# Graph attention on one core: softmax inside tiles of 128 edges, with 0/1 matrices that ScalarE forms, in place of scans that run over all edges

## What is computed

```
L0:  dinv = rsqrt(degree);  w = dinv[row] * dinv[col]
     h = x;  x_out = 0.1 x;  five times: h = segment_sum(h[col] * w, row);  x_out += 0.18 h
     x = layernorm(x + x_out @ W0.T + b0)
L1:  q = (x @ Wq)                                     # n x 8 heads x 8
     k = ((x[src] * (sh @ Wang_k.T)) @ Wlin_k) * (relu(ea @ W1k + b1k) @ W2k)     # e x 8 x 8
     v = ((x[src] * (sh @ Wang_v.T)) @ Wlin_v) * (relu(ea @ W1v + b1v) @ W2v)     # e x 8 x 16
     alpha = einsum('ehq,qk,ehk->eh', q[dst], Wdot, k)
     attn  = softmax of alpha over the edges of one dst, per head
     x = layernorm(x + segment_sum(attn * v, dst) @ Wout)
```

## Time and profile before

| | |
|---|---|
| median of 3 runs | 7642.49 us (7631.2 to 7643.73) |
| profiled execution, its span | 7626.3 us |
| instructions | 100,942 |
| PE busy | 5985.3 us (78%) |
| VectorE (DVE) busy | 4953.3 us (65%) |
| GpSimd (POOL) busy | 3561.9 us (47%) |
| ScalarE (ACT) busy | 2725.1 us (36%) |
| `edge_attention`, first transpose to the issue of the last store | 3311.0 to 7451.0 us |

### The profile page before, as it was taken

How to read it: one execution, slowest core, us unless ns; L and a number is a source line. 1 busy time by engine, 2 the same in 40 slices (tenths; PEclk the granted TensorE clock), 3 DMA queues, 4 the chain that set the end, 5 groups by cost and what they waited for, 6 DMA issues and landing times. The chain is left out here.

```text
span 7626.3 us, 100942 instructions
## 1 busy us (share of the span) xinstructions
PE 5985.3 (78%) x25186; PEld 2930.0 (38%) x25186; DVE 4953.3 (65%) x6867; ACT 2725.1 (36%) x5068; POOL 3561.9 (47%) x3216
## 2 busy tenths in 40 slices
PE   3444599999999998358888888888888888888883
PEld 3444444444444444323333333333333333333331
DVE  5555611111111112369999999999999999999994
ACT  3443411111111111234444444444444444444441
POOL 2222110000000000267777777777777777877773
PEclk7666799999999999578988888888898899998885
DMA  5666769687877867034444443444434444443441
GB/s 104 104 102 104 109 224 314 207 289 235 262 251 240 280 215 267 21 83 112 111 111 110 110 113 108 112 111 110 112 110 109 113 110 110 112 112 108 113 104 39
DMA packets 1158275, 1100.52 MB, mean 144 GB/s; under 512 B 569810, under 2 KB 997180, under 8 KB 1158092
## 3 DMA queue, kind: packets, MB, share of 16 engines
q1 hardware_dynamic: 753548, 752.46, 36.0%
q10 hardware_dynamic: 344208, 218.52, 8.9%
q0 software_dynamic: 60336, 127.10, 6.2%
HBM read 791.60 MB, written 305.95 MB: 144 GB/s over the span
## 5 line engine op out<-in xcount | busy, mean ns | idle before, releaser
L2025 POOL DMA_INDIRECT e_x_rows<-x_table,e_src_ix x1616 | 2007.2, 1242 | 525.8 <-issue 512.9
L1154 PE MATMUL acc<-t_ring,scaled 128*128 128x512 f16 (+1 forms) x9555 | 1966.5, 368 | 56.4 <-ACT scaled L1173 46.1
L1154 PEld LDWEIGHTS acc<-t_ring,scaled 128*128 128x128 bf16 x9555 | 907.4, 98 | 1100.9 <-issue 76.3
L2095 PE MATMUL e_b_gv<-e_prod,e_head_sum 64*128 64x512 f32 x808 | 524.4, 734 | 682.3 <-DVE e_x_gv L2206 679.2
L1250 POOL TENSOR_TENSOR less_two<-less_one,scaled 128x512 f32<-128x512 f32 (+1 forms) x65 | 71.9, 1106 | 1759.6 <-ACT scaled L1173 1759.6
L534 PE MATMUL lists_rows_ps<-lists_hot_lo,lists_hot_hi 128*128 128x196 fp8e4 x3200 | 436.9, 313 | 463.4 <-DVE lists_hot_hi L459 463.3
L2037 POOL TENSOR_TENSOR e_lift<-e_lift,e_top 128x512 f32<-128x512 f32 x404 | 577.1, 1429 | 31.7
L534 PEld LDWEIGHTS lists_rows_ps<-lists_hot_lo,lists_hot_hi 128*128 128x128 fp8e4 x3200 | 378.6, 122 | 517.9 <-DVE lists_hot_hi L459 482.4
L2053 PE MATMUL e_b_lk<-e_x_gk,e_wlin_k 128*64 128x512 f32 x808 | 576.8, 804 | 0.0
L2034 POOL TENSOR_TENSOR e_lift<-e_fresh,e_top 128x512 f32<-128x512 f32 x404 | 442.8, 1096 | 284.7 <-DVE e_top L2251 268.8
L2157 ACT COPY e_out_rows<-e_b_o 128x512 f32<-128x512 f32 x404 | 236.2, 585 | 871.9 <-PE e_b_gk L2105 871.9
(11 more groups left out here) (173 smaller groups left out, 8881.5 us busy)
## 6 DMA issues: line engine op xcount, KB each, us to landing
t_ring<-adjacency_half SPq DMA_DIRECT2D x245, 800.0 KB, 7.0
t_ring<-adjacency_half SPq DMA_DIRECT2D x245, 768.0 KB, 4.3
sums_table<-e_out_rows ACTq DMA_DIRECT2D x404, 272.0 KB
e_same_dst<-same_row SPq DMA_DIRECT2D x404, 256.0 KB, 3.7
adjacency_half<-lists_staged SPq DMA_DIRECT2D x196, 392.0 KB, 8.3
q_first<-hop_zeros_q ACTq DMA_DIRECT2D x101, 512.0 KB, 8.6
e_q_rows<-q_first SPq DMA_DIRECT2D x404, 128.0 KB
parts_sh<-e_part ACTq DMA_DIRECT2D x404, 64.0 KB, 4.4
```

The source lines that it names most:

```text
L1154: mm = nc.tensor.matmul(acc[c][:, 0:n], U[p][:, b, :], ring[m % RING][:, lo:lo + n], start=(b == 0 and p == 0), stop=(b == NB - 1 and p == 2),
L2025: nc.gpsimd.indirect_dma_start(x_rows[s][:, j, :], None, x1_table, bass.IndirectOffsetOnAxis(ap=src_ix[s][:, j:j + 1], axis=0)).then_inc(x ...
L2095: nc.tensor.matmul(b_gv[:], head_sum[:], prod[o][:], start=True, stop=True).then_inc(p_score, 1)
```

## The change

- Edges are taken in pairs of groups, group i of the first half of the edge list beside group i + 202 of the second half: 202 pairs (`N`), written out without a loop (`ITERATIONS`), the values running seven pairs behind (`LAG`). Work with 64 partitions is stacked, one group in the lower and one in the upper 64.
- Scores of four pairs (`BATCH`) are put on the 128 partitions (4 pairs x 4 tile positions x 8 heads) with two tiles of 128 edges along the free axis. Maximum and sum are found by scans inside one tile of 128 edges (`find_most` forward and backward, `add_weights` backward), 256 columns each per four pairs. The flags `neg` and `keep` come from two new tables in HBM.
- Values are formed with edges on partitions: `values` and `radial_values` are 8 matmuls of 128 columns each whose stationary operand is the edges' data, and VectorE multiplies straight from PSUM (`weigh`, `finish_values`).
- The sum over the edges of a segment inside a tile is a matmul (`spread_out`) with a 128 x 128 matrix of zeros and ones per tile, which ScalarE forms in two steps (`find_spots`): |spot - column| for each of 8 tiles, then relu(1 - that) over all 1,024 columns. `fpos`, the position in its tile at which an edge's segment starts, comes from a new block, `locate_edges`.
- `sh` and `ea` are cut into two float32r parts in place of three bfloat16 parts.
- The stores move from ScalarE's queue to SyncE's. GpSimd's two `lift` operations are gone; its gathers stay, 8 per pair.
- `attention_output` merges segments that cross tiles: it loads the first row of each tile, scans over the 1,616 tiles, writes `next_table`, gathers `rows` and then `more` (49 indirect DMAs each) and adds the two. `node_layer` gets one more gather and store for the query at the middle edge. `clear_spent` lets semaphores be used again.

The core of the diff:

```
-BIG = 1.0e30
-ROW = D + H
+BIG = 2.0 ** 100
+ROW = D + 2 * H
...
+        locate_edges(nc, a, spent, ident, first_edge, last_edge, has_edges, fpos, q_place, row_first, row_next,
+                     neg_table, keep_table, NB, G)
...
+    BATCH = 4
+    LAG = 7
+    VR = 8
+    XR = 3
+    K = 2 * GT
...
+        turn_ps = ctx.enter_context(nc.psum_tensor("e_turn_ps", [P, 2, GE], F32))
+        ring_ps = [ctx.enter_context(nc.psum_tensor(f"e_ring_ps{s}", [P, 2, GE], F32)) for s in range(2)]
...
+            def spread_out(j, i):
+                pe.wait_ge(v_weighted, j + 1)
+                pe.wait_ge(a_spot, j + 1)
+                if i < N:
+                    pe.wait_ge(a_hid, i + 1)
...
+                for k in range(K):
+                    mm = nc.tensor.matmul(turn_ps[:, k // GT, k % GT * P:(k % GT + 1) * P], spot[j % 2][:, k, :],
+                                          weighted[j % 2][:, k, :], start=True, stop=True)
+                mm.then_inc(p_seg, 1)
...
+            def keys_and_radial(i):
...
+                for g in range(2):
+                    mm = nc.tensor.matmul(bank[g * 64:(g + 1) * 64, 1, :], w2k[g * 64:(g + 1) * 64, :],
+                                          hid_k[s][g * 64:(g + 1) * 64, :], start=True, stop=True)
+                mm.then_inc(p_rk, 1)
+                for g in range(2):
+                    mm = nc.tensor.matmul(bank[g * 64:(g + 1) * 64, 0, :], wlin_k[:], x_gk[s][:, g, :],
+                                          start=True, stop=True)
+                mm.then_inc(p_lk, 1)
...
+            def hidden(r):
...
+                pe.wait_ge(a_xt, r + 1)
+                for n in range(2):
+                    mm = nc.tensor.matmul(turn_ps[:, n, :], stack[:, (2 + n) * D:(3 + n) * D], ea[s][:],
+                                          start=True, stop=True)
+                mm.then_inc(p_hid, 1)
...
+            for i in ITERATIONS:                     # TensorE
+                j = i - LAG
+                if on(j - 1):
+                    spread_out(j - 1, i)
+                if on(i - 1):
+                    scores(i - 1)
+                if chain_at(i - 2) is not None:
+                    turn_weights(chain_at(i - 2), i)
+                if on(j):
+                    values(i, j)
+                    radial_values(i, j)
+                if on(i + 1):
+                    turn_x(i + 1, i)
+                if on(i):
+                    keys_and_radial(i)
+                if on(i + 1):
+                    hidden(i + 1)
+                    turn_q(i + 1)
+                    gates(i + 1)
...
+            def find_spots(j):
+                if j >= 1:
+                    act.wait_ge(a_spot, j)
+                for k in range(K):
+                    nc.scalar.activation(gap[:, k, :], iota[:], ACT.Abs, bias=fpos[:, j * K + k:j * K + k + 1],
+                                         scale=-1.0).then_inc(a_gap, 1)
+                act.wait_ge(a_gap, K * (j + 1))
+                if j >= 2:
+                    act.wait_ge(p_seg, j - 1)
+                nc.scalar.activation(spot[j % 2][:], gap[:], ACT.Relu, bias=ones[:, 0:1], scale=-1.0).then_inc(a_spot, 1)
...
+            for i in ITERATIONS:                     # ScalarE
+                if on(i - LAG - 1):
+                    keep_rows(i - LAG - 1)
+                if chain_at(i - 2) is not None:
+                    keep_weights(chain_at(i - 2))
+                if on(i + 1):
+                    keep_x(i + 1)
+                    keep_hidden(i + 1)
+                if on(i - LAG):
+                    find_spots(i - LAG)
...
```

More of the change, by code:

```diff
@@ L55, in semaphores, with clear_spent @@
     return sem
+def clear_spent(eng, spent):
+    nums = sorted(spent)
+    while nums:
+        n = 1
+        while n < len(nums) and nums[n] == nums[0] + n:
+            n += 1
+        eng.sem_clear(range(nums[0], nums[0] + n))
+        del nums[0:n]
+    spent.clear()
 def first(k):
@@ new lines, in edge_attention @@
+        by_head = sb("by_head", [P, 2 * H])
+        head_sum = sb("head_sum", [P, BATCH, 8 * H])
+        iota_i = sb("iota_i", [P, P], I32)
+        iota = sb("iota", [P, P])
+        src_ix = sb("src_ix", [P, G * GT], I32)
+        x_rows = [sb(f"x_rows{s}", [P, K, D]) for s in range(XR)]
+        q_rows = pair("q_rows", [P, GT, 2, DQ])
+        sh = pair("sh", [P, GE], FR)
+        ea = pair("ea", [P, GE], FR)
+        same = pair("same", [P, GE])
+        x_t = pair("x_t", [P, 2, GE])
+        q_t = pair("q_t", [P, GE])
@@ L1993, in _ @@
+            load(1)
+            for i in ITERATIONS:
+                if on(i - LAG - 1):
+                    store(i - LAG - 1)
+                if i >= 0 and i % BATCH == 0 and i // BATCH < NBATCH:
+                    load_flags(i // BATCH)
+                if i >= 0 and on(i + 2):
+                    load(i + 2)
+            for s in range(2):
+                sp.wait_ge(stored[s], 16 * len(range(s, N, 2)))
         @block.gpsimd
         def _(pool):
-            nc.gpsimd.memset(w2k[:], 0.0).then_inc(const, 1)
@@ new lines, in turn_weights @@
+            def turn_weights(n, i):
+                pe.wait_ge(a_exp, n + 1)
+                pe.wait_ge(v_lsum, n + 1)
+                if i < N:
+                    pe.wait_ge(a_hid, i + 1)
+                if i - LAG - 1 >= 0:
+                    pe.wait_ge(a_out, i - LAG)
+                if n >= 1:
+                    pe.wait_ge(a_wt, 3 * n)
+                for c, src in enumerate((weight, most, lsum)):
+                    for v in range(2):
+                        at = c % 2 * 2 * P + v * P
+                        tr = nc.tensor.transpose(turn_ps[:, c // 2, at:at + P], src[:, v * P:(v + 1) * P], ident[:])
+                tr.then_inc(p_wt, 1)
@@ new lines, in scores @@
+            def scores(i):
+                n, p = divmod(i, BATCH)
+                pe.wait_ge(v_prod, i + 1)
+                if p == 0 and n >= 1:
+                    pe.wait_ge(v_drop, n)
+                by_half = prod[i % 2][:].rearrange("r (v u e) -> r u v e", v=2, u=2)
+                for u in range(2):
+                    mm = nc.tensor.matmul(
+                        score_ps[u * 64:(u + 1) * 64, :].rearrange("r (v e) -> r v e", v=2),
+                        head_sum[:, p, :], by_half[:, u, :, :], start=(p == 0),
+                        stop=(p == BATCH - 1 or i == N - 1), skip_group_check=True)
+                mm.then_inc(p_score, 1)
@@ new lines, in gates @@
+            def gates(r):
+                s = r % 2
+                pe.wait_ge(sh_in[s], 32 * (r // 2 + 1))
+                for n, done in enumerate((p_gk, p_gv)):
+                    bank = ring_bank(5 * r + n)
+                    for g in range(2):
+                        rows = slice(g * 64, (g + 1) * 64)
+                        mm = nc.tensor.matmul(bank[:, g, :], stack[rows, n * D:(n + 1) * D], sh[s][rows, :],
+                                              start=True, stop=True)
+                    mm.then_inc(done, 1)
@@ new lines, in _ @@
+            chain(nc.vector.tensor_tensor(fall[0][:], rows[:, :, D:D + H], peak[:], ALU.subtract))
+            chain(nc.vector.tensor_tensor(fall[1][:], more[:, :, D:D + H], peak[:], ALU.subtract))
+            for n, src in enumerate((rows, more)):
+                dve.wait_ge(exped, n + 1)
+                chain(nc.vector.tensor_tensor(part[n][:], src[:, :, D + H:ROW], scale[n][:], ALU.mult))
+            chain(nc.vector.tensor_tensor(total[:], part[0][:], part[1][:], ALU.add))
+            chain(nc.vector.reciprocal(inverse[:], total[:]))
```

1246 lines of the change are left out of this document (773 added, 473 removed).

## The result

The kernel after took 7099.5 us in the median (7086.3 to 7112.6) against 7642.5: a ratio of 0.929 [0.927, 0.931]. Forecast were 7043. Measured again unchanged (e9), beside the kernel before in the same session (7640.7), it took 7044.7 (7038.8 to 7047.4), ratio 0.9226 [0.9211, 0.9242]. So the first measurement was some 50 us long. Part of the difference shows in its profile: the first `spread_out` starts at 3431.0 us, in the second profile at 3401.5, though the node layer ahead of it is 3 us earlier; in between engines wait for a releaser that the trace only calls remote. Why is open. The experiments were taken on two chips, on which the kernel before took from 7608 to 7641 us; so they stand beside the second measurement by their ratios, and not by their times.

A forecast was written before the change was run, and what follows sets the result against it. A TensorE-ScalarE ring was taken to bound the attention: 10.31 / 0.87 + 4.95 = 16.8 us a turn, loop 3,425. Span 7626.3 - 4140 + 3425 + 116 = 7027, plus 16 gives 7043 us; range 6590 to 7440.

The forecast's parts named there:

- The ring: Attention loop: TensorE from spread_out to hidden, then ScalarE's keep_hidden and find_spots, back to spread_out; 16.8 us a turn.
- ScalarE's part: In each attention turn: keep_hidden 1.28 plus find_spots 3.67, together 4.95 us.
- TensorE's part at full clock: In each attention turn, spread_out through hidden: 11.38 us summed, 10.31 after partial overlap of pairs in separate array halves.
- rival 1: Attention matmul pairs run wholly side by side: TensorE's part 8.35, turn 14.55, time 6604 us; chance 0.22.
- The clock: TensorE's granted clock in the attention, lowered by one longer stand per pair: 0.87, applied to TensorE's 10.31 us.
- The price of float32r: TensorE matmul of 512 float32r columns: taken as 0.21 us, at most 0.86; the dear end adds 1.3 us a pair.
- The rest of the attention: Attention loop total: 195 full turns of 16.8 us plus 149 us for first and last turns, 3,425 in place of 4,140.
- What is added elsewhere: Outside the attention loop: locate_edges 30, node_layer 5, attention_output 81 us; together 116 us.
- What was to show it: Profile signs: turn about 17 us, VectorE under half, GpSimd about 60%, e_spot wait about 3.5 us, clock 0.8 to 0.9.
- Rival 2: Attention matmul pairs lie in no way side by side: turn 18.0, loop 3,665, time about 7280 us; chance 0.22.
- Rival 3: TensorE's low clock decides and the kernel gets slower; gain gone at a turn of 19.9 us; chance 0.12.
- Rival 4: ScalarE is quicker, so GpSimd's gathers bind instead of the ring: turn 12.3 us, time about 6170; chance 0.04.

The follow-up runs named there:

- e9: Kernel after measured again unchanged, beside the kernel before in the same session; 7044.7 us, ratio 0.9226.
- e1: Kernel after with find_spots placed ahead of keep_x and keep_hidden in ScalarE's turn; 5918.8 us, ratio 0.7775.
- e3: Kernel after with ten useless float32r matmuls of 512 columns on TensorE while ScalarE finds the spots; 6540.6 us, ratio 0.8592.
- e10: Kernel after with three extra ScalarE relus of 512 columns per turn, between gaps and spots; 7393.0 us, ratio 0.9686.
- e11: Kernel after with six extra ScalarE relus of 512 columns per turn, between gaps and spots; 7829.3 us, ratio 1.0258.
- e12: e1 with the two halves of the radial keys separated by both halves of the linear keys on TensorE; 6088.9 us, ratio 0.7976.
- e7: e1 with the 16 passes of radial_values ordered by row half instead of by turns; 6023.5 us, ratio 0.7894.
- e13: e1 with the o_heads load in attention_output cut into two, of 96 and 5 partitions; 6684.1 us, ratio 0.8776.
- e6: Kernel after with two extra VectorE products of 512 columns per turn, into scratch behind the query scan; 7036.9 us, ratio 0.9221.
- e4: Kernel after with the 16 passes of radial_values ordered by row half instead of by turns; 7011.8 us, ratio 0.921.
- e5: Kernel after with one extra ScalarE relu of 512 columns per turn, between gaps and spots; 7049.8 us, ratio 0.9236.

## Why the prediction was right

The predicted 7043 us stand against 7099.5 at first and 7044.7 when measured again, so the total is right, and the chain behind it too. The terms of the sum were less right than the sum, and that e9 lies within 2 us of the forecast is luck. Against the sum, e9's loop takes 25 us more and `attention_output` 27 more, the hops take 27 less and the other blocks some 7 less, which is 18 us more in the span; and e9's median lies 1 us below its profiled span, where the sum put it 16 above.

**The ring** was named in full, and e1, e3, e10 and e11 confirm it from both sides: take ScalarE's work out and 3.2 us a turn go, put 3.8 in and 3.8 come.

**ScalarE's part**: 4.95 forecast, 4.91 measured. `find_spots` 3.67 in the sum; in the timeline 5028.79 to 5032.51 is 3.72.

**TensorE's part at full clock**: 10.31 forecast, 9.73 measured (e3). Here two errors met. The rule taken for pairs in separate halves (three steps of four for the keys and scores, nothing for `radial_values`) failed: e12 has both halves in the time of one, e7 puts 0.55 us on the radial pairs. That is rival 1's mechanism. But rival 1's 8.35 was too low as well, because single steps are dearer than I made them from their rows: `spread_out` 1.95 us and `values` 1.98 from start to start (1.76 each in the sum), `turn_x` 1.02 (0.88), a pair of keys 1.01 (0.86), `scores` 0.58 (0.43), `radial_values` 1.09 (0.88), `hidden` to its end 0.73 (0.59). So rival 1 was right in mechanism and 1.38 us short in price. The Trainium skill (TensorE: Matmul & The Clock Gate, Part 3) has matmuls in separate row or column groups run concurrently; e12 agrees where rows and columns are separate, 1.01 us for two halves and 1.00 for one; e7 in part where only the rows are, 1.09 for 1.64.

**The clock**: 0.87 taken, over TensorE's part 9.73 / 12.15 = 0.80 by the times; the stage's row says 0.80 too, and the granted clock over TensorE's part alone is 0.77 (mean of the 160 turns). It costs 2.42 us a turn and not 1.54. I had set it from the share of low clock in the stage before, spread evenly over the work; but it falls once a turn, in the stand, in the median 1.2 us before its end (e9), and stays low over `spread_out`, `scores` and the first part of `values`. Windows in the turn shown above:

```profile
5015.50:5021.30 5.80, 5.75 (x24) 4.80 (x25) 0.00 (x0) 1.47 (x3) 1.89 (x2) 0.50 0.15 37
5021.30:5031.50 10.20, 7.59 (x55) 4.70 (x54) 7.75 (x8) 4.84 (x12) 4.81 (x5) 1.00 0.63 186
```

The whole cost thus lies on the work right behind the stand. 0.58 too much on one term and 0.88 too little on the other make 0.30 us, 17.07 for 16.8: two errors of opposite sign.

**The price of float32r**, 0.21: ten of 512 columns take 2.57 us in e3, the last of them 0.40 by their mean length, so 2.17 / 9 = 0.24 each. Right within 0.1 us for the two of a turn.

**The rest of the attention.** From block to block the attention takes 4170 us before and 3480 in e9 (3511 in the first profile): 690 less, 715 forecast. The longer turn alone is 195 x 0.26 = 51 us; the other 26 are less time in the head and tail than the 149 us of the sum.

**What is added elsewhere.** `locate_edges` 24 us (30 forecast), `node_layer` 1 (5). `attention_output` is the step that was mis-sized most: 119 us more than before in the first profile and 108 in e9, 81 forecast. I had laid the scans, with their loads and transposes, some 45 us, under the first gathers. In the kernel after:

```profile
6840.71 2.85 PE L2628 MATMUL o_head_ps<-ident,o_heads 101*8 101x101 f32 x16 [52.42 <-DMA o_heads<-sums_table]
...
6886.35 0.38 SPq L2596 DMA_DIRECT2D next_table<-o_next_rows  x1
```

```profile
L2617 POOL DMA_INDIRECT o_more<-next_table,row_next x49 | 46.2, 944 | 49.0 <-DMA next_table<-o_next_rows 34.4 <-issue 14.6
```

The load alone, issued at 6793.06, takes 47.6 us and the work behind it another 46, so the second gathers wait 34.4 us for the table (20.3 in e9). e13 shows that the load of 101 partitions was the slow part. Against this the hops take 2063 us (982 to 3045) in place of 2096 (952 to 3048), 33 us for which the sum had no term; from the first matmul of the hops to the last it is 32 us less, and 27 in e9. TensorE's busy time is 9 us less there and its idle time 24. I had left the lighter cutting of `sh` and `ea` at nothing; that it is the cause is likely but not shown, as no run took it apart.

**What was to show it.** The turn of 17 us, VectorE under half, the wait for `e_spot` of 3.5 us, the clock of 0.8 and the close starts of the keys are all there. GpSimd is 44% busy where I wrote about 60: I had counted the 0.30 us of issue at each gather, with which it is 10.0 of 17.07 us. The 98 gathers of `attention_output` take 158 us (6794.1 to 6952.1) and not 125, by the wait told above.

**The rivals.** Rival 2 is excluded by e7 and e12. Rival 3 named the right cost: the clock takes 14% of the turn. It does not reach 19.9 us unless ScalarE's part nearly doubles, as e11 does. Rival 4 is excluded by the gathers' 7.2 us of wait a turn, but it is near: at e1's 10.8 us in an ordinary turn they need 10.0.

## What to carry to other kernels

When no engine is near full (here TensorE is busiest, at 77%), follow one wait after another until you come back to the first: in the ring, look for work that is queued behind something it does not need, and move it. Two lines moved in ScalarE's order were worth 0.145 of the time before, some 1,110 us, almost twice what the whole change had brought (0.077). And price a stand of TensorE twice: once as the wait, once as the low clock of the work behind it, here 3.6 and 2.4 us.

## What was not expected of the hardware

A pair of float32 matmuls of 512 columns in separate row and column halves costs 1.01 us, one half alone 1.00 (e12); 16 passes of 128 columns in row halves take 1.09 us by turns and 1.64 half by half (e7). A float32r matmul of 512 columns takes 0.24 us at full clock (e3).

A gather takes 953 ns beside a VectorE that is 45% busy (after) and beside one that is 67% busy (e1), and 1,244 in the kernel before, where VectorE is 95% busy and GpSimd has other work too. 1.38 us of products of two SBUF tiles a turn make it 972 (e6). Which part of the 1,244 comes of VectorE no run takes apart.

With the stand in the turn, small additions on TensorE (e4, 0.55 us) or ScalarE (e5, 0.61 us) do not lengthen it: 17.06 or 17.07 us in all of after, e4, e5, e6 and e9, as the low clock then covers less of TensorE's work (0.84 in e4 and 0.83 in e5 over the attention, 0.80 in e9). A dose test near such a state says "not on the path" of something that is on it; only larger doses told the truth.

One instruction more on another engine's queue, in a later block, came with 3.7 us more a turn in the attention (e13), in part in pauses between TensorE's matmuls that no semaphore explains; the cause is open. Whoever tries a small edit and finds it far slower should look at a stage that the edit does not touch.
